# First attention of a graph and feed-forward kernel made ahead of the gathers, five units to four steps, and causal logits made first where it is done

## The chip, the cores and the metric

The kernel runs on one core of a Trainium2 chip, as one program. The metric is device time in microseconds. Five engines work side by side, each through its own list of instructions in order: TensorE (PE in the rows, its weight loads PEld), VectorE (DVE), ScalarE (ACT), GpSimd (POOL, which here issues gathers only) and SyncE (SP, which issues all other transfers). They wait for each other by semaphores.

## The reference, cut to what matters

Four residual layers run over `x`, 2048 nodes of 128 channels: a graph attention with curvature, a product-key feed-forward with causal attention, a second graph attention, and a mixture of experts. The change lies in the first two, which the kernel does in one stage:

```python
x = x + _L0_gnn_ref(_layernorm(x), positions, curv_feats, adj, W, a_l, a_r, Wc, gate)
x = x + _L0_ffn_ref(_layernorm(x)[None], Wq_pk, pk_keys, Wq, keys_table, values_table, Wo)[0]
...
# first: logits over all 2048 nodes for 8 heads, masked by adj, softmax, weigh h
logits = leaky_relu(e_l[:, None, :] + e_r[None, :, :]) + gate * curv_bias
out = einsum('ijh,jhd->ihd', softmax(where(mask, logits, -1e9), axis=1), h)
...
# second: per head, 16 rows of a table of keys and one of values chosen by two top-16 lists,
# summed with softmax weights; then causal attention over the 2048 nodes with them
k = einsum('bnhk,bnhkd->bnhd', kv_scores, keys_table[ind])
v = einsum('bnhk,bnhkd->bnhd', kv_scores, values_table[ind])
attn = softmax(where(causal, einsum('bihd,bjhd->bhij', q, k), neg))
out = einsum('bhij,bjhd->bhid', attn, v)
```

## The kernel before, in words

The stage is the function `curvature_keys_and_attention`. The nodes are cut into 16 tiles of 128 (T = 16), and everything is done for 8 heads (H = 8).

**Units of first attention.** The first attention is cut into 128 units of 16 nodes and all 8 heads (KU = 8 units a tile). A unit u needs: its logits (TensorE, eight matmuls into the four banks of `psL`, L548 and L552), a relu part and a difference (ScalarE, L722 and L729), their sum and row-maximum (VectorE, `max_of`, L863 to L868), the exponential (ScalarE, L734), four rounds of turning (TensorE, L559), copying (ScalarE, L742) and weighing (TensorE, L567), and a scaled pick (VectorE, L873 and L875). The logits of the next unit are made ahead of the weighing of this one. After the eighth unit of a tile the picks are folded and added to X (L629, L1049), the tile is normalised and turned into `row_xT` (L1053 to L1060, L686, L815), and the next block of the adjacency is converted (`turn_adj`, L854).

**Steps of gathering.** From tile 1 on, each step (t, k) also serves head k of tile t - 1: TensorE makes a query (L643) and the similarities (L652), VectorE finds the 16 rows (`choose`, L907 to L968), POOL gathers them, 16 indirect transfers to a step (L508), into a ring that holds two steps' rows. Two steps later (LAG = 2) VectorE sums them with their weights (L993, L997, L1006, L1007). TensorE turns the summed key (L660), and ScalarE copies it (L796). SP stores key and value to device memory.

**Causal attention.** In step x = 12 + w (BEHIND = 12), head w of the causal attention is taken up (w counts 8 heads to a tile): query (L573, copy L756), logits in `psL` (`attend`, L585 and L587) over up to 16 blocks, maximum on VectorE (L880), exponential on ScalarE (L766), and in the next step `at_head`: turning (L592), copying (L749), weighing with the values (L604), then a projection (`project`, L620), which VectorE adds to X (L889). SP fetches the values (L468) and keys (L461) of a head from device memory.

**Order.** The program is written out in full, 18 rounds of `tile` with 8 steps each: 144 steps, x = 8t + k. Rounds 0 to 15 hold first attention, one unit a step; rounds 1 to 16 choose and gather; heads of causal attention lie at steps 12 to 139. So steps 0 to 7 hold first attention alone, and steps 128 to 143 none. No planner orders the work: each engine goes through its own list in the order of its `tile` function, for TensorE in a step with everything: query, logits of the next unit, similarities, causal query, turn of a key, `at_head` of the last head, `attend` of this one, `project`, and turning and weighing of this unit. VectorE: last sums' weights and the first 8 slots, pick of the last unit, maximum of the next, choosing with the causal maximum in it, the other slots.

Of the kernel before, what the change touches and what calls it, by code (L numbers as in the profile page):

```python
# [6 lines left out]
C = 128  # L7
P = 128
T = N // P
H = 8  # L10
# [179 lines left out]
BEHIND = H + LAG + 2  # L190


def curvature_keys_and_attention(nc, ins, X, ident, big_ident, psL, psT, psV, psO, keysT_out, values_out, adj_out):
# [28 lines left out]
    with ExitStack() as ctx:  # L222
# [59 lines left out]
        row_xT = sb("row_xT", [C, 4, P])  # L282
# [135 lines left out]
        with nc.Block() as block:  # L418
            @block.sync
            def _(sp):  # L420
# [49 lines left out]
                def tile(t, s1, last, choosing, adding):  # L470
                    if s1:
                        sp.wait_ge(adj_turned, t + 1)
                        if not last:
                            sp.dma_start(adj_raw[:, :], adj_v[:, t + 1, :]).then_inc(adj_loaded, 16)
                        sp.dma_start(adj_out[t, :, :], adj_neg[:, :]).then_inc(adj_stored, 16)
                    for k in range(H):
# [12 lines left out]
                        if v is not None:  # L489
                            fetch_keys(v)  # L490

                each_tile(tile)
# [20 lines left out]
            def _(pe):  # L513
# [23 lines left out]
                def logits_of(t, k, first=False):  # L537

                    u = KU * t + k
                    if not first:  # L540
                        pe.wait_ge(mx_ready, u)
                    if k == 0:
                        pe.wait_ge(adj_turned, t + 1)
                    v = attended(t, k - 1)
                    if v is not None and v >= 1:
                        pe.wait_ge(at_probs_ready, v)
                    for c in range(NC):
                        nc.tensor.matmul(psL[:, c * CH:(c + 1) * CH], spread[:, k, :],  # L548
                                         adj_neg[:, c * CH:(c + 1) * CH], start=True, stop=False)
                        if c == 0:  # L550
                            pe.wait_ge(diff_ready, u + 1)
                        last = nc.tensor.matmul(psL[:, c * CH:(c + 1) * CH], bias_w[:, :],  # L552
                                                bias_rhs[:, k % 2, c * CH:(c + 1) * CH], start=False, stop=True)
                    last.then_inc(logits_ready, 1)
# [8 lines left out]
                def weigh(t, k, q):  # L563
                    pe.wait_ge(probsT_ready, 4 * (KU * t + k) + q + 1)
                    for s in range(4):
                        j = 4 * q + s
                        last = nc.tensor.matmul(psV[:, k % 2, :], probsT[:, q % 2, s, :], vals[:, j, :],  # L567
# [4 lines left out]
                def query(t, v):  # L572
                    nc.tensor.matmul(psT[:, 1, 2 * NK:2 * NK + P], at_wq[:, v % H, :], row_xT[:, t % 4, :],  # L573
                                     start=True, stop=True).then_inc(at_q_done, 1)

                def attend(v, u):
# [3 lines left out]
                    pe.wait_ge(mx_ready, min(u + 2, UNITS))  # L580
# [15 lines left out]
                def at_weigh(v, q):  # L596
                    pe.wait_ge(at_probsT_ready, quarters_to(v) + q + 1)
                    if q == 0:
# [3 lines left out]
                        pe.wait_ge(x_added, min(T, (v + 1 + BEHIND) // H))  # L602
# [6 lines left out]
                def at_head(v):  # L609
# [3 lines left out]
                    for q in range(n):  # L613
                        if q + 1 < n:
                            at_turn(v, q + 1)
                        at_weigh(v, q)
# [6 lines left out]
                def fold_in(t):  # L623
                    pe.wait_ge(picked_ready, KU * (t + 1))
                    v = attended(t, KU - 1)
                    if v is not None:
                        pe.wait_ge(at_added, v)
# [5 lines left out]
                def tile(t, s1, last, choosing, adding):  # L633
                    for k in range(H):
                        v = H * (t - 1) + k
                        u = KU * t + k
                        w = attended(t, k)
                        if choosing:
                            if k == 0:
                                pe.wait_ge(xT_ready, t)  # L640
                            if not s1:
                                pe.wait_ge(key_copied, v - LAG - 1)
                            nc.tensor.matmul(psT[:, 0, 0:P], wq[:, k, :], row_xT[:, (t - 1) % 4, :],  # L643
                                             start=True, stop=True).then_inc(qT_done, 1)
                        if s1:
                            if k < KU - 1:
                                logits_of(t, k + 1)
                            elif not last:
                                logits_of(t + 1, 0)
                        if choosing:  # L650
                            pe.wait_ge(qT_copied, v + 1)
                            nc.tensor.matmul(psT[:, 1, 0:2 * NK], qT[:, :], keys[:, k, :],  # L652
                                             start=True, stop=True).then_inc(sim_done, 1)
                        if w is not None:
                            query(w // H, w)
                        if turns_key(t, k, choosing, adding):
                            pe.wait_ge(total_ready, v - LAG)
                            if not choosing:
                                pe.wait_ge(key_copied, v - LAG - 1)
                            nc.tensor.transpose(psT[:, 0, 0:P], total[:, :], ident[:, :]).then_inc(key_turned, 1)  # L660
                            pe.wait_ge(key_copied, v - LAG)
                        if choosing:
                            pe.wait_ge(sim_copied, v + 1)
                        if w is not None:
                            pe.wait_ge(at_q_ready, w + 1)
# [5 lines left out]
                        if s1:  # L671
                            pe.wait_ge(probs_ready, u + 1)
                            turn(0)
                            turn(1)
                            if u >= 1:
                                pe.wait_ge(picked_ready, u)
                            weigh(t, k, 0)
                            turn(2)
                            weigh(t, k, 1)
                            turn(3)  # L680
                            weigh(t, k, 2)
                            weigh(t, k, 3)
                    if s1:
                        fold_in(t)
                        pe.wait_ge(xn_ready, t + 1)
# [8 lines left out]
                logits_of(0, 0, first=True)  # L694
                each_tile(tile)
                at_head(H * T - 1)
# [3 lines left out]
            def _(act):  # L700
# [17 lines left out]
                def relu_of(t, k):  # L718
                    u = KU * t + k
                    if u >= 1:  # L720
                        act.wait_ge(probs_ready, u)
                    nc.scalar.activation(relu_part[:, :], er_rows[:, :], ACT.Relu,  # L722
                                         bias=el_cols[:, bass.ds(u, 1)], scale=1.0 - SLOPE).then_inc(relu_ready, 1)

                def diff_of(t, k):
# [968 lines left out]
```

## Time and profile before

| what | value |
|---|---|
| median of 3 runs | 4347.53 us (4346.95 to 4349.38) |
| the profiled execution | 4337.04 us |
| its span, first to last instruction | 4335.3 us |
| busy in the span: TensorE, VectorE, ScalarE, POOL | 3470.9, 3336.2, 2284.3, 2049.0 us |
| mean granted clock of TensorE, of full speed | 0.918 |
| the stage of the change | until about 2998 us |

Busy time is the time in instructions; what an engine spends on issuing transfers, waiting and branching isn't in it, so POOL's share says little about how close its gathers follow one another. A row of a timeline gives the start, the busy time, the engine, the line, the operation and the tiles, the count of the merged instructions, and in brackets the idle time ahead and what ended it. The granted clock is a share of 2.4 GHz; 0.5 is 1.2 GHz, and a value in between is a mean over a stretch that had both.

### The profile page before, as it was taken

How to read it: one execution, taken by the hardware profiler on the slowest of the kernel's cores; microseconds unless marked ns; L12 is line 12 of the kernel's file. 1: busy time of each engine (PE TensorE's matmuls, PEld its weight loads, DVE VectorE, ACT ScalarE, POOL GpSimd, SP SyncE). 2: the span in 40 equal slices, each digit the busy share in tenths (PEclk: the TensorE clock that was granted, in tenths of full speed). 3: DMA queues.
4: the chain of work that ended last, by engine and by line, in shares of the span. 5: the costliest groups of instructions: out<-in, count | busy, mean ns of one | idle time of the engine just before them, and what ended most of it. 6: DMA issues, size and time to landing. Idle time of an engine off the chain costs nothing. (4 is left out here: it accounts for less than half of the span.)

```text
span 4335.3 us, 62381 instructions
## 1 busy us (share of the span) xinstructions
PE 3470.9 (80%) x19465; PEld 2679.8 (62%) x19592; DVE 3336.2 (77%) x10591; ACT 2284.3 (53%) x3657; POOL 2049.0 (47%) x2052
## 2 busy tenths in 40 slices
PE   6867777777778788888888989566888888888797
PEld 4645555555555565566666666445677777777575
DVE  2679889899898898898988989663877777777334
ACT  5645455555555555565555655222656666665232
POOL 0377777777777777777766767660000000000000
PEclk9988889999999999999999999777999999999799
DMA  2244444554555555555555556554000000000100
GB/s 75 61 128 118 133 139 134 146 153 141 156 149 162 168 170 174 170 179 176 180 180 184 189 168 205 171 181 160 1 1 1 1 1 1 1 1 1 41 0 10
DMA packets 187672, 477.90 MB, mean 110 GB/s; under 512 B 43933, under 2 KB 87137, under 8 KB 182881
## 3 DMA queue, kind: packets, MB, share of 16 engines
q0 software_dynamic: 98304, 268.57, 21.4%
q1 hardware_dynamic: 89052, 205.52, 14.0%
q8 instruction: 151, 2.47, 0.2%
q14 instruction: 165, 1.34, 0.1%
HBM read 447.57 MB, written 26.21 MB: 109 GB/s over the span
## 5 line engine op out<-in xcount | busy, mean ns | idle before, releaser
L508 POOL DMA_INDIRECT ck_ring<-in_tables,ck_rows x2048 | 2048.8, 1000 | 879.4 <-issue 751.3
L993 DVE SCALAR_TENSOR_TENSOR ck_part<-ck_ring,ck_norm_w,ck_part 128x256 f32<-128x256 f32 x1792 | 768.7, 475 | 62.5 <-DVE ck_rows L968 41.7
L567 PE MATMUL psV<-ck_vals,ck_probsT 128*128 128x128 f32 x4096 | 554.2, 284 | 112.3 <-ACT ck_probsT L742 105.8
L552 PE MATMUL psL<-ck_bias_rhs,ck_bias_w 110*128 110x512 f32 x1024 | 571.7, 641 | 87.0 <-ACT ck_bias_rhs L729 38.4
L567 PEld LDWEIGHTS psV<-ck_vals,ck_probsT 128*128 128x128 f32 x4096 | 501.8, 196 | 161.3 <-ACT ck_probsT L742 92.0
L1204 PE MATMUL psL<-ga_probsT,ga_vals 128*128 128x256 f32 x2048 | 528.1, 405 | 0.7 <-ACT ga_probsT L1301 0.7
L742 ACT COPY ck_probsT<-psT 128x512 f32<-128x512 f32 x512 | 281.3, 587 | 443.5 <-PE psT L559 439.1
L1204 PEld LDWEIGHTS psL<-ga_probsT,ga_vals 128*128 128x128 f32 x2048 | 398.7, 205 | 51.6 <-ACT ga_probsT L1301 0.9
L1191 PE MATMUL psT<-ident,ga_probs 128*128 128x128 f32 x2048 | 303.0, 283 | 153.8 <-ACT ga_probsT L1301 149.5
L1191 PEld LDWEIGHTS psT<-ident,ga_probs 128*128 128x128 f32 x2048 | 248.8, 146 | 204.4 <-issue 184.1
L1292 ACT ACTIVATE ga_probs<-ga_probs,ga_neg_mx 128x2048 f32<-128x2048 f32 x128 | 256.5, 2004 | 220.9 <-DVE ga_neg_mx L1352 220.5
L1301 ACT COPY ga_probsT<-psT 128x512 f32<-128x512 f32 x512 | 281.3, 585 | 162.9 <-PE psT L1191 162.3
L585 PE MATMUL psL<-ck_keysT,ck_at_qT 128*128 128x512 f32 (+3 forms) x640 | 270.5, 555 | 91.7 <-DVE ck_neg_mx L868 91.5
L604 PE MATMUL psO<-ck_at_probsT,ck_values 128*128 128x128 f32 x2176 | 308.2, 291 | 41.5 <-ACT ck_at_probsT L749 41.5
L604 PEld LDWEIGHTS psO<-ck_at_probsT,ck_values 128*128 128x128 f32 x2176 | 276.3, 201 | 71.2 <-ACT ck_at_probsT L749 71.2
L552 PEld LDWEIGHTS psL<-ck_bias_rhs,ck_bias_w 110*128 110x128 f32 x1024 | 213.1, 208 | 165.5 <-issue 145.6
L559 PE MATMUL psT<-ident,ck_probs 128*128 128x128 f32 x2048 | 305.4, 285 | 3.1 <-ACT ck_sim L786 2.7
L1342 DVE SCALAR_TENSOR_TENSOR ga_probs<-ga_s_rows,ga_s_cols,ga_s_slope 128x2048 f32<-128x2048 f32 x128 | 300.3, 2346 | 6.6 <-ACT ga_s_slope L1274 6.0
L1346 DVE CUSTOM_DVE_ANT_0 ga_probs<-ga_probs,ga_adj_neg 128x2048 f32<-128x2048 f32 x128 | 292.6, 2286 | 5.4
L864 DVE CUSTOM_DVE_ANT_0 ck_relu_part<-psL,ck_relu_part 128x2048 f32<-128x2048 f32 x128 | 292.8, 2287 | 0.5 <-issue 0.5
L749 ACT COPY ck_at_probsT<-psT 128x512 f32<-128x512 f32 (+3 forms) x320 | 159.0, 524 | 206.3 <-PE psT L592 206.3
L734 ACT ACTIVATE ck_probs<-ck_relu_part,ck_neg_mx 128x2048 f32<-128x2048 f32 x128 | 257.8, 2014 | 16.1 <-DVE ck_neg_mx L868 16.1
(205 smaller groups left out, 5616.0 us busy)
## 6 DMA issues: line engine op xcount, KB each, us to landing
ck_ring<-in_tables,ck_rows POOLq DMA_INDIRECT x2048
ck_adj_raw<-in_adj SPq DMA_DIRECT2D x16, 1024.0 KB, 9.5
adj_scratch<-ck_adj_neg SPq DMA_DIRECT2D x16, 512.0 KB
values_scratch<-ck_values_tile SPq DMA_DIRECT2D x128, 64.0 KB, 1.7
keysT_scratch<-ck_keys_tile SPq DMA_DIRECT2D x128, 64.0 KB
ck_keysT<-keysT_scratch SPq DMA_DIRECT2D x8, 1024.0 KB
ck_values<-values_scratch SPq DMA_DIRECT2D x8, 1024.0 KB
ga_adj_neg<-adj_scratch SPq DMA_DIRECT2D x16, 512.0 KB, 11.9
```

What stands on the lines that cost most here:

```text
L508: pool.indirect_dma_start(ring[:, slot, :], None, ins["tables"], bass.IndirectOffsetOnAxis(rows[:, k, s:s + 1], axis=0)).then_inc(got[(u * ...
L552: last = nc.tensor.matmul(psL[:, c * CH:(c + 1) * CH], bias_w[:, :], bias_rhs[:, k % 2, c * CH:(c + 1) * CH], start=False, stop=True)
L559: last = nc.tensor.transpose(psT[:, q % 2, s * P:(s + 1) * P], probs[:, j * P:(j + 1) * P], ident[:, :])
L567: last = nc.tensor.matmul(psV[:, k % 2, :], probsT[:, q % 2, s, :], vals[:, j, :], start=(j == 0), stop=(j == T - 1))
L604: last = nc.tensor.matmul(psO[:, P:2 * P], values[:, j, :], at_probsT[:, q % 2, j % 4, :], start=(j == 0), stop=(j == blocks(v) - 1))
L742: nc.scalar.copy(probsT[:, q % 2, :, :].rearrange("p s c -> p (s c)"), psT[:, q % 2, :]).then_inc(probsT_ready, 1)
L864: nc.vector.tensor_tensor_reduce(out=logits[:, :], in0=psL[:, :], in1=relu_part[:, :], scale=1.0, scalar=-3.0e38, op0=ALU.add, op1=ALU.max ...
L993: done.append(c.did(nc.vector.scalar_tensor_tensor(part[:, s % 2, :], ring[:, slot, :], norm_w[:, s:s + 1], part[:, s % 2, :], ALU.mult, A ...
L1191: last = nc.tensor.transpose(psT[:, q % 2, s * P:(s + 1) * P], probs[:, u % 3, j * P:(j + 1) * P], ident[:, :])
L1204: last = nc.tensor.matmul(out, vals[:, k % 2, j, :], probsT[:, g % 2, j, :, :].rearrange("p h i -> p (h i)"), start=(j == 0), stop=(j == T ...
L1342: nc.vector.scalar_tensor_tensor(probs[:, u % 3, :], s2_rows[:, k % 2, :], s1_cols[:, t, k:k + 1], s2_slope[:, k % 2, :], ALU.add, ALU.max ...
L1346: nc.vector.tensor_tensor_reduce(out=probs[:, u % 3, :], in0=probs[:, u % 3, :], in1=adj_neg[:, t, :], scale=1.0, scalar=-3.0e38, op0=ALU.add,
```

## The change: what it does

- The order is written over units instead of tiles. Round 0 is as before. In rounds 1 to 16 each fourth step is followed by an extra unit, which does first attention alone, as long as units are left. So five units of first attention go to four steps of gathering; the last unit (127) is the extra one behind step 103, and steps 104 to 143 have none.
- Where a step has no first attention (`g is None`), TensorE makes the causal logits of this head (`attend`) right behind the causal query, ahead of the turn of the key and of `at_head` of the last head. In the other steps the order is as before.
- Normalised tiles are kept eight deep (`KEPT`) instead of four, since they are made further ahead.
- SP loads and stores an adjacency block behind the unit that ends a tile, instead of ahead of the next tile's first step.
- Columns of the biases are read at constant places instead of through a register's slice. `opening` is False throughout, so what hangs on it is not done.

```diff
+EVERY = 4
+KEPT = 8
...
-        row_xT = sb("row_xT", [C, 4, P])
+        row_xT = sb("row_xT", [C, KEPT, P])
...
-        def each_tile(tile):
-
-            for t in range(T + 2):
-                tile(t, s1=t < T, last=t >= T - 1, choosing=1 <= t <= T, adding=2 <= t <= T + 1)
+        def each_unit(unit):
+
+            g = 0
+            for x in range(H * (T + 2)):
+                t, k = x // H, x % H
+                unit(t, k, g if g < UNITS else None, choosing=1 <= t <= T, adding=2 <= t <= T + 1, extra=False)
+                g = min(g + 1, UNITS)
+
+                if 1 <= t <= T and x % EVERY == EVERY - 1 and g < UNITS:
+                    unit(t, k, g, choosing=False, adding=False, extra=True)
+                    g += 1
...
+                def keep_adj(j):
+                    sp.wait_ge(adj_turned, j + 1)
+                    if j + 1 < T:
+                        sp.dma_start(adj_raw[:, :], adj_v[:, j + 1, :]).then_inc(adj_loaded, 16)
+                    sp.dma_start(adj_out[j, :, :], adj_neg[:, :]).then_inc(adj_stored, 16)
...
+                    if g is not None and g % KU == KU - 1 and g + 1 < UNITS:
+                        keep_adj(g // KU + 1)
...
-                        pe.wait_ge(x_added, min(T, (v + 1 + BEHIND) // H))
+                        if folds(g) >= 1:
+                            pe.wait_ge(x_added, folds(g))
...
+                def unit(t, k, g, choosing, adding, extra):
+                    v = H * (t - 1) + k
+                    w = None if extra else attended(t, k)
+                    issued = (attended(t, k) or 0) + (1 if extra and attended(t, k) is not None else 0)
+                    more = g is not None and g + 1 < UNITS
+                    opening = False
+                    if folds(g) >= 1:
+                        pe.wait_ge(xT_ready, folds(g))
+                    if choosing:
+                        if g is None:
+                            pe.wait_ge(key_copied, v - LAG - 1)
+                        nc.tensor.matmul(psT[:, 0, 0:P], wq[:, k, :], row_xT[:, (t - 1) % KEPT, :],
+                                         start=True, stop=True).then_inc(qT_done, 1)
+                    if more and not opening:
+                        logits_of(g + 1, issued)
+                    if choosing:
+                        pe.wait_ge(qT_copied, v + 1)
+                        nc.tensor.matmul(psT[:, 1, 0:2 * NK], qT[:, :], keys[:, k, :],
+                                         start=True, stop=True).then_inc(sim_done, 1)
...
+                    if w is not None:
+                        query(w // H, w)
+                    if w is not None and g is None:
+                        attend(w, g)
+                    if turns_key(t, k, choosing, adding):
+                        pe.wait_ge(total_ready, v - LAG)
...
+                    if w is not None:
+                        pe.wait_ge(at_q_ready, w + 1)
+                        if g is None:
                             if w >= 1:
-                                at_head(w - 1)
-                            attend(w, u)
+                                at_head(w - 1, g)
+                        else:
                             if w >= 1:
-                                project(w - 1)
...
+                                at_head(w - 1, g)
+                            attend(w, g)
+                        if w >= 1:
+                            project(w - 1)
+                    if g is not None:
+                        pe.wait_ge(probs_ready, g + 1)
+                        turn(0)
+                        turn(1)
+                        if g >= 1:
+                            pe.wait_ge(picked_ready, g)
+                        weigh(g, 0)
...
+                    if g is not None and g % KU == KU - 1:
+                        fold_in(g // KU, attended(t, k))
...
+                    if summing is not None:
+                        norm_weights(*summing)
+                        add_slots(TOP - BESIDE if g is not None else 2)
+                    if g is not None and g % KU >= 1:
+                        pick(g - 1)
+                    if more and not opening:
+                        max_of(g + 1)
+                    w = None if extra else attended(t, k)
```

The lists of ScalarE and VectorE follow the same loop: in an extra unit ScalarE does relu, difference, four copies and an exponential, VectorE a pick and a maximum, and where a unit ends a tile, the tile's end as before.

## Rows read from the trace of the kernel before

**Rows 1.** Windows of the stage; columns: PE, PEld, DVE, ACT, POOL, PEclk, DMA share, GB/s

```profile
161.00:2170.00 2009.00, 1578.83 (x8786) 1163.66 (x8881) 1780.95 (x6630) 1096.28 (x1824) 1523.23 (x1518) 0.93 0.51 153
2170.00:2712.00 542.00, 477.26 (x2844) 357.15 (x2867) 473.08 (x1676) 317.09 (x511) 381.36 (x384) 0.97 0.57 185
2712.00:2907.00 195.00, 115.53 (x542) 90.06 (x540) 135.55 (x508) 49.49 (x109) 128.76 (x132) 0.72 0.54 178
```

**Rows 2.** Timeline of POOL, its last two gathers

```profile
2926.45 0.95 POOL L508 DMA_INDIRECT ck_ring<-in_tables,ck_rows  x1 [0.30 <-issue]
2927.71 0.95 POOL L508 DMA_INDIRECT ck_ring<-in_tables,ck_rows  x1 [0.30 <-issue]
```

**Rows 3.** Line L508, all gathers: who waited for them (us, times)

```profile
  DVE ck_part L993: 20.7, 12
```

**Rows 4.** Timeline of VectorE in an ordinary step

```profile
1232.57 0.15 DVE L873 RECIPROCAL ck_rinv<-ck_rsum 128x1 f32<-128x1 f32 x1
1233.03 2.29 DVE L864 CUSTOM_DVE_ANT_0 ck_relu_part<-psL,ck_relu_part 128x2048 f32<-128x2048 f32 x1
...
1235.44 0.49 DVE L907 MAX8 ck_best<-ck_sim 128x8 f32<-128x128 f32 x2
...
1252.54 2.28 DVE L864 CUSTOM_DVE_ANT_0 ck_relu_part<-psL,ck_relu_part 128x2048 f32<-128x2048 f32 x1
```

**Rows 5.** Timeline of TensorE in the same step

```profile
1223.69 2.05 PE L567 MATMUL psV<-ck_vals,ck_probsT 128*128 128x128 f32 x16 [1.35 <-ACT ck_probsT L742]
...
1229.26 1.02 PE L552 MATMUL psL<-ck_bias_rhs,ck_bias_w 110*128 110x512 f32 x2
```

**Rows 6.** Timeline of TensorE in tile 0, a unit with nothing beside it

```profile
104.92 1.02 PE L552 MATMUL psL<-ck_bias_rhs,ck_bias_w 110*128 110x512 f32 x2
...
109.02 1.04 PE L559 MATMUL psT<-ident,ck_probs 128*128 128x128 f32 x8
...
115.17 1.02 PE L552 MATMUL psL<-ck_bias_rhs,ck_bias_w 110*128 110x512 f32 x2
```

**Rows 7.** Timeline of VectorE, row-maxima of four units around a tile's end

```profile
933.61 2.29 DVE L864 CUSTOM_DVE_ANT_0 ck_relu_part<-psL,ck_relu_part 128x2048 f32<-128x2048 f32 x1
...
957.72 2.29 DVE L864 CUSTOM_DVE_ANT_0 ck_relu_part<-psL,ck_relu_part 128x2048 f32<-128x2048 f32 x1
...
986.60 2.29 DVE L864 CUSTOM_DVE_ANT_0 ck_relu_part<-psL,ck_relu_part 128x2048 f32<-128x2048 f32 x1
...
1005.68 2.29 DVE L864 CUSTOM_DVE_ANT_0 ck_relu_part<-psL,ck_relu_part 128x2048 f32<-128x2048 f32 x1
```

**Rows 8.** Timeline of VectorE, rows chosen in step 103 and in step 135

```profile
2169.59 1.04 DVE L968 TENSOR_REDUCE ck_rows<-ck_hit 128x16 uint32<-128x864 f32 x1
...
2906.62 1.04 DVE L968 TENSOR_REDUCE ck_rows<-ck_hit 128x16 uint32<-128x864 f32 x1
```

**Rows 9.** Timeline of a step without first attention, VectorE and TensorE

```profile
2783.93 2.16 DVE L880 TENSOR_REDUCE ck_at_neg_mx<-psL 128x1 f32<-128x1920 f32 x1 [6.15 <-PE psL L587]
...
2795.25 0.47 PE L660 MATMUL psT<-ident,ck_total 128*128 128x128 f32 x1 [5.25 <-DVEq L173]
...
2796.13 1.97 PE L592 MATMUL psT<-ident,ck_at_probs 128*128 128x128 f32 x8 [0.41 <-ACT ck_keys_tile L796]
...
2802.67 3.39 PE L585 MATMUL psL<-ck_keysT,ck_at_qT 128*128 128x512 f32 x8
...
2806.15 2.16 DVE L880 TENSOR_REDUCE ck_at_neg_mx<-psL 128x1 f32<-128x1920 f32 x1 [4.53 <-PE psL L587]
```

**Rows 10.** Timeline of SP's queue in the same step

```profile
2802.91 0.32 SPq L468 DMA_DIRECT2D ck_values<-values_scratch  x1
...
2806.19 0.32 SPq L461 DMA_DIRECT2D ck_keysT<-keysT_scratch  x1
```

**Rows 11.** Window of one microsecond, columns as in rows 1

```profile
2813.00:2814.00 1.00, 0.00 (x0) 0.00 (x0) 0.97 (x3) 0.10 (x1) 0.59 (x1) 0.50 0.12 45
```

**Rows 12.** Timeline of VectorE, the stage's last addition to X

```profile
2997.09 0.35 DVE L889 SCALAR_TENSOR_TENSOR X<-psO,ck_at_rinv,X 128x128 f32<-128x128 f32 x1 [9.40 <-PE psO L620]
```

More of the change, by code:

```diff
@@ L468, in fetch_values @@
                     sp.dma_start(values[:, 0:n, :], values_out[v % H, :, 0:n, :]).then_inc(values_in, 16)
[L470 to L476, printed above, removed]
+                def keep_adj(j):
[4 more added lines that the diff above has]
+                def unit(t, k, g, choosing, adding, extra):
+                    if not extra:
                         n = H * t + k - (BEHIND - 1)
@@ L631, in fold_in @@
                     last.then_inc(folded, 1)
[L633 to L665, printed above, removed]
@@ L693, in _ @@
                 pe.wait_ge(at_in, 48)
-                logits_of(0, 0, first=True)
-                each_tile(tile)
-                at_head(H * T - 1)
+                logits_of(0)
+                each_unit(unit)
+                at_head(H * T - 1, None)
                 project(H * T - 1)
@@ L822, in _ @@
+                        nc.scalar.copy(row_xT[:, g // KU % KEPT, :], psT[:, 0, 0:P]).then_inc(xT_ready, 1)
+                relu_of(0)
+                diff_of(0)
+                diff_of(1)
+                exp_of(0)
+                each_unit(unit)
                 at_copy(H * T - 1)
@@ L855, in turn_adj, with max_of @@
                                             ALU.is_gt, ALU.add).then_inc(adj_turned, 1)
[L857 to L859 removed]
+                def max_of(u):
+                    if u >= 1:
                         dve.wait_ge(probs_ready, u)
@@ new lines, in unit, with add_slots, attend_now @@
+                def unit(t, k, g, choosing, adding, extra):
+                    more = g is not None and g + 1 < UNITS
+                    opening = False
+                    if more and g % KU == KU - 1:
+                        turn_adj(g // KU + 1)
+                    summing = summed(t, k, choosing, adding)
+                    done = []
+                    def add_slots(n):
+                        if summing is not None:
+                            for s in range(len(done), min(len(done) + n, TOP)):
+                                add_slot(*summing, s, done)
+                    if summing is not None:
[5 more added lines that the diff above has]
+                        max_of(g + 1)
+                    w = None if extra else attended(t, k)
+                    def attend_now():
+                        if w is not None:
+                            attend(w)
+                    if choosing:
+                        choose(t - 1, k, not adding and k == 0, add_slots, summing is not None, attend_now)
+                    else:
+                        attend_now()
+                    if more and opening:
+                        max_of(g + 1)
+                    if summing is not None:
+                        add_slots(TOP)
+                        finish_sums(*summing, adding or k > LAG, done)
+                    if g is not None and g % KU == KU - 1:
+                        tile = g // KU
+                        pick(g)
+                        dve.wait_ge(folded, tile + 1)
+                        nc.vector.tensor_tensor(X[:, tile, :], X[:, tile, :], psO[:, 0:P], ALU.add).then_inc(x_added, 1)
+                        dve.wait_ge(x_added, tile + 1)
@@ L1064, in _ @@
                 dve.wait_ge(keys_in, 64)
-                max_of(0, 0, first=True)
-                each_tile(tile)
+                max_of(0)
+                each_unit(unit)
                 add_head(H * T - 1)
```

245 lines of the change are left out of this document (102 added, 143 removed).

## The prediction

> **What bounds the kernel now.** I read the stages first, by windows [rows 1]. The change touches the stage up to 2998 us and nothing behind it. For most of that stage, 161 to 2170 us, VectorE is busy 1781 us of 2009 (89%), TensorE 1579 (79%), ScalarE 1096 (55%), and POOL 1523 (76%). POOL's share misleads: the gap between two gathers isn't counted as busy. Start to start, two gathers in a row are 1.26 us apart [rows 2], so 16 cost about 20.1 us without a pause. A step (one gathered head) takes some 21 us on average. POOL is therefore nearly full too. But who waits for whom? VectorE waited for a gather only 20.7 us in the whole run, in 12 places [rows 3]. So it is VectorE's own order, not POOL, that sets the pace of most steps, with POOL close behind it.
>
> Inside an ordinary step VectorE has no hole worth naming: from one row-maximum (L864) at 1233.03 to the next at 1252.54 is 19.5 us [rows 4]. TensorE is ahead of it there: its last weighing ends at 1223.69 + 2.05 = 1225.7, the next unit's logits are done at 1229.26 + 1.02 = 1230.3, and VectorE comes for them only at 1233.03 [rows 4, 5]. TensorE is thus 2.8 us early, no more.
>
> **Part 1: 24 units of first attention without a gather.** From step 8 on, five units go to four steps, so the 120 units that are left after tile 0 take 96 steps and 24 extra passes. What an extra pass costs is seen in tile 0, where units run with nothing beside them: logits start at 104.92, turning at 109.02, the next unit's logits at 115.17 [rows 6], that is 10.25 us of TensorE for a unit, 4.1 for logits and 6.15 for turning and weighing, with ScalarE's copies between. An extra pass puts these 10.25 us in TensorE's order behind the weighing at 1225.7, at 1236.0; the step's own logits need 4.5 us behind that (1225.7 to 1230.3), so the row-maximum that was at 1233.03 comes at 1240.5, 7.5 us later. VectorE's extra work (pick and maximum, 1232.57 to 1235.44, 2.9 us [rows 4]) fits into that. ScalarE's share of such a unit does too: it kept up with the 10.25 us in tile 0, and 55% leave it room. Bounds: 2.9 us, if only VectorE's work counted, and 10.25, if TensorE had no lead. I take 7.5, as rows 4 to 6 give it directly: 24 x 7.5 = +180 us.
>
> **Part 2: tile ends come earlier.** Every eighth unit ends a tile: fold, layer norm, turning, a new adjacency block. Row-maxima around one are at 933.61, 957.72, 986.60 and 1005.68 [rows 7]: 24.1 and 28.9 us against 19.1 of the plain step behind them, so 14.8 us for a tile's end, most of it waiting (VectorE's fold, norm and adjacency block are short). Before, step 103 had begun the end of tile 12 (counted from 0); now all sixteen are over by then. Three and two thirds of an end move ahead of step 104: +54 us here, and they come off the stretch of part 3, whose old time holds them. Bounds: 0, if extra passes filled all of it, and 54.
>
> **Part 3: steps 104 to 135 carry no first attention.** Their rows came from 2169.59 to 2906.62 [rows 8], 737.0 us or 23.0 a step. In the last eight of them, which had no first attention before either, a step takes 2806.15 - 2783.93 = 22.2 us, of which VectorE waits 4.5 to 6.2 for causal logits [rows 9]. The chain there: sums done, key turned at 2795.25, at_head (turn and weigh) from 2796.13, logits from 2802.67, maximum at 2806.15. The second part of the change takes the logits ahead of the key's turning, so VectorE no longer waits: its own work is 22.2 - 4.5 = 17.7 us. Who is late next? POOL, at 20.1 us a step; and a new loop: keys are fetched right behind the values once weighing ends (2802.91 before, the keys at 2806.19 [rows 10]). The two transfers are over by 2813, where the DMA's share has fallen to 0.12 [rows 11], 10.2 us after the weighing. Add logits (3.4), key turn and copy (0.9) and at_head (6.5): 21.0 us at 15 blocks, less with fewer. Bounds: 20.1 (POOL) and 22.2 (no gain). I take 21.0: 32 x 21.0 = 672, so -65 us. Queued behind the logits' new place are the key's turn, at_head and project, and ScalarE and SP wait for these; that wait is in the loop.
>
> **Part 4: the ends.** At the start VectorE's 20.7 us of waiting for gathers [rows 3] lie in the first steps, where two or three extra passes fall: -21 (bounds 0 and -21). Behind the last gather (2927.71 [rows 2]) the stage runs on to 2997.09 [rows 12], 69 us in which VectorE waits for causal logits; the new order shortens each of four heads by a few us: -10 (bounds 0 and -24). SP's adjacency load and store now stand behind a step's four transfers instead of ahead of them; what they wait for is done by then, and the next block is needed six steps later: 0. Eight kept row blocks in place of four, and constants in place of a register for the columns: 0, no wait of before names them.
>
> **The sum:** 180 + 54 - 21 - 65 - 10 = **+138 us**. The profiled execution took 4337.0 us (span 4335.3 and 1.7 around it), so 4475; the runs' median of 4347.5 is 10.5 above that execution, so **4485 us** on the runs.
>
> **Rivals.** *Cheap passes.* TensorE's pass might hide wholly, so that an extra unit costs VectorE's 2.9 us alone: 24 x 2.9 = 70 in place of 180, +28, 4376 us. For it: VectorE is the busiest engine [rows 1]. Against: TensorE's lead is 2.8 us and the pass takes 10.25 [rows 4 to 6]. The Trainium skill, Perfetto Trace Analysis, "Identifying the Most-Contended Engine", says that the engine with the highest occupancy is the one that limits; by that rule this rival would hold, and the trace agrees with it only for plain steps. 13%.
>
> *VectorE never waits (faster).* As the last, and the waits at tile ends are filled as well, since an extra pass now stands beside some of them: ends cost 0 in place of 54, sum 70 - 21 - 65 - 10 = -26, 4321 us. The place is VectorE's wait between the last weighing of a tile and the next maximum. It decides if an extra pass with its share of a tile's end costs under (21 + 65 + 10) / 24 = 4.0 us; I have 9.8. For it: up to 14.8 us at each end [rows 7]. Against: TensorE's order is fixed, and only three extra passes stand directly ahead of the last unit of a tile. 7%.
>
> *TensorE alone in the freed steps is slow.* The granted clock is 0.72 in the stretch without first attention against 0.93 and 0.97 ahead of it [rows 1], a mixture of 1.2 and 2.4 GHz; eight transposes take 1.97 us here [rows 9] and took 1.04 in tile 0 [rows 6]. If the loop of part 3 runs at the lower, its 10 us of TensorE grow by several, the freed steps gain only what was bounded above (-26), the tail nothing, and if TensorE's lead is used up elsewhere the passes cost 10.25: 246 + 54 - 21 - 26 = +253, 4600 us. The Trainium skill, TensorE: Matmul & The Clock Gate, "Part 1: The HAM clock gate (the 'warmup' mystery)", calls the half rate the default that only activity lifts; that speaks against taking work away from TensorE, and the rows of this stretch agree. 15%.
>
> *It does not do what it says.* Excluded: 8 + 5 x 24 = 128 units by step 103, written out by the program's own loop.
>
> **How the numbers follow.** My own case has 65%, and its range is 4430 to 4540 (an extra pass at 6 to 9 us, freed steps at 20.1 to 22). The range must hold 8 in 10: down to the cheap passes, and up into the slow case: 4370 to 4580. About 0.2% (8.7 us) is what a measurement of this kernel can tell from no change. Faster needs the second rival: 7%. Within 0.2% needs something between the first rival and the second: 4% of the 13% of cheap passes. The rest, 65 + 15 + 9 = 89%, is slower.
>
> **What would show it.** Right: in steps 8 to 103 VectorE waits 3 to 5 us for psL by L552's line in each extra pass, POOL shows pauses for rows (L971's queue) where it had none, and gathers end later than 2927.7 by some 150 us; from step 104 on POOL runs again nearly without pause, and the wait for L587's line is gone. Wrong: no wait of VectorE in an extra pass (cheap passes), or steps of 22 us and more after 104 with waits for keys (slow case). If POOL stays without pauses up to step 103, the sum falls at part 1.

## The result and the profile after

| | before | after |
|---|---|---|
| median of the runs, us (4 each, side by side) | 4347.92 (4346.95 to 4349.38) | 4465.52 (4461.28 to 4468.62) |
| span of the profiled execution | 4335.3 | 4464.5 |
| its own time | 4337.0 | 4466.2 |
| rows chosen in step 103 | 2169.59 | 2375.14 |
| rows chosen in step 135 | 2906.62 | 3035.16 |
| last gather starts | 2927.71 | 3078.27 |
| last addition to X | 2997.09 | 3128.57 |

The changed kernel is slower: its time is 1.027 times that of before (95% interval 1.0252 to 1.0287), 118 us. 4485 was forecast, with 4370 to 4580 as the range.

The page of the changed kernel: the span, the engines' busy time and the gathers.

```profile
span 4464.5 us, 62417 instructions
...
PE 3527.0 (79%) x19465; PEld 2680.7 (60%) x19592; DVE 3339.3 (75%) x10591; ACT 2284.9 (51%) x3657; POOL 2048.3 (46%) x2052
...
L525 POOL DMA_INDIRECT ck_ring<-in_tables,ck_rows x2048 | 2048.1, 1000 | 1030.7 <-issue 761.2
```

The work is the same, 2048 gathers of 1000 ns on average; what grew is the idle time between them. Where it grew, the windows by stage show (columns as in [rows 1]; the stages end where step 103, step 135 and the stage end now).

```profile
161.00:2375.00 2214.00, 1806.29 (x10209) 1333.56 (x10327) 1856.21 (x6806) 1287.81 (x2020) 1514.24 (x1518) 0.94 0.47 140
2375.00:3036.00 661.00, 422.44 (x1979) 286.06 (x1977) 538.38 (x2023) 178.64 (x424) 500.37 (x499) 0.78 0.59 193
3036.00:3129.00 93.00, 59.38 (x295) 41.73 (x295) 30.67 (x67) 21.78 (x39) 33.48 (x33) 0.78 0.42 146
```

POOL has some 1515 us of gathers up to step 103, as before [rows 1], in 2214 us in place of 2009. In the stretch without first attention it is busy 500 us of 661 (76%), which is close to no pause at all, as [rows 2] said.

VectorE's timeline in the changed kernel, the choice of rows (L992, L968 before) in steps 23, 103, 104 and 135, then the last addition to X:

```profile
486.80 1.04 DVE L992 TENSOR_REDUCE ck_rows<-ck_hit 128x16 uint32<-128x864 f32 x1
...
2375.14 1.05 DVE L992 TENSOR_REDUCE ck_rows<-ck_hit 128x16 uint32<-128x864 f32 x1
...
2405.58 1.05 DVE L992 TENSOR_REDUCE ck_rows<-ck_hit 128x16 uint32<-128x864 f32 x1
...
3035.16 1.05 DVE L992 TENSOR_REDUCE ck_rows<-ck_hit 128x16 uint32<-128x864 f32 x1
...
3128.57 0.35 DVE L913 SCALAR_TENSOR_TENSOR X<-psO,ck_at_rinv,X 128x128 f32<-128x128 f32 x1 [10.50 <-PE psO L636]
```

Against [rows 8] and [rows 12]: step 103 comes 205.5 us later, step 135 only 128.5 later, and the stage ends 131.5 later. So 205.5 us go to steps 8 to 103, 77 come back in steps 104 to 135, and 3 go to what follows. Of the 205.5, 2.1 were there before the first extra unit: the rows of step 8 are chosen at 165.07 in the profiled execution of before and at 167.20 in this one.

**An extra pass.** VectorE's row-maxima (L888) about an ordinary extra unit of the changed kernel, the one behind step 55; the second is the one that VectorE makes in the extra unit:

```profile
1215.55 2.29 DVE L888 CUSTOM_DVE_ANT_0 ck_relu_part<-psL,ck_relu_part 128x2048 f32<-128x2048 f32 x1
...
1232.00 0.06 DVE L887 MEMSET ck_waited<- 128x1 f32 x1 [0.58 <-PE psL L567]
1232.04 2.29 DVE L888 CUSTOM_DVE_ANT_0 ck_relu_part<-psL,ck_relu_part 128x2048 f32<-128x2048 f32 x1
...
1242.46 0.06 DVE L887 MEMSET ck_waited<- 128x1 f32 x1 [4.10 <-PE psL L567]
1242.51 2.29 DVE L888 CUSTOM_DVE_ANT_0 ck_relu_part<-psL,ck_relu_part 128x2048 f32<-128x2048 f32 x1
```

The stretch takes 27.0 us with the extra unit in it. Row-maxima of plain steps are 19.1 to 19.5 us apart [rows 4, 7], so this unit cost 7.5 to 7.9 us. TensorE over the same time:

```profile
1225.47 2.05 PE L582 MATMUL psV<-ck_vals,ck_probsT 128*128 128x128 f32 x16 [1.22 <-ACT ck_probsT L762]
1227.57 1.02 PE L567 MATMUL psL<-ck_bias_rhs,ck_bias_w 110*128 110x512 f32 x2
...
1231.67 1.04 PE L574 MATMUL psT<-ident,ck_probs 128*128 128x128 f32 x8
1233.03 1.13 PE L582 MATMUL psV<-ck_vals,ck_probsT 128*128 128x128 f32 x8 [0.33 <-ACT ck_probsT L762]
...
1235.77 2.00 PE L582 MATMUL psV<-ck_vals,ck_probsT 128*128 128x128 f32 x16
...
1238.04 1.02 PE L567 MATMUL psL<-ck_bias_rhs,ck_bias_w 110*128 110x512 f32 x2
```

From one unit's logits (1227.57) to the next's (1238.04) it is 10.47 us with hardly a hole; the pass was costed at 10.25 from [rows 6]. VectorE, 2.8 us behind TensorE in the plain step [rows 4, 5], now waits for it, here 0.58 + 4.10 us. ScalarE does not hold the pass up: TensorE waits 0.33 us for one of its copies, and its copies wait 2.35 us for TensorE (0.35, 1.26 and 0.74). All such waits up to step 103, first before, then after (columns: who waits, for what; us in total, times, longest):

```profile
DVE ck_waited L863 <- PE psL L552: 78.8, 23, 5.5
...
POOL ck_ring L508 <- DVEq L992: 36.2, 64, 5.4
```

```profile
POOL ck_ring L525 <- DVEq L1016: 250.6, 79, 20.4
...
DVE ck_waited L887 <- PE psL L567: 207.7, 62, 8.5
```

VectorE waits 129 us longer for first logits, and POOL, which had no pause to speak of, stands 214 us longer behind VectorE's queue: the two signs that the prediction named for part 1. It named the line that hands over rows for the second one (L971, now L995), and the trace puts the pauses down to the line that frees places of the ring (L1016). The gather that ends a long pause starts 2.0 us behind a choice of rows, though (step 56: rows at 1254.0, and the gather at 1256.0, 5.3 us behind the one before it).

**A freed step.** Steps 104 to 135 run differently: TensorE, VectorE and POOL of the changed kernel in one of them.

```profile
2869.46 5.10 PE L600 MATMUL psL<-ck_keysT,ck_at_qT 128*128 128x512 f32 x8 [0.76 <-DMA ck_keysT<-keysT_scratch]
```

```profile
2880.18 0.62 DVE L1021 TENSOR_SCALAR ck_part<-ck_ring,ck_norm_w 128x256 f32<-128x256 f32 x2 [4.69 <-DMA ck_ring<-in_tables,ck_rows]
```

```profile
2877.54 0.95 POOL L525 DMA_INDIRECT ck_ring<-in_tables,ck_rows  x1 [0.30 <-issue]
2878.80 0.94 POOL L525 DMA_INDIRECT ck_ring<-in_tables,ck_rows  x1 [0.30 <-issue]
2880.04 0.95 POOL L525 DMA_INDIRECT ck_ring<-in_tables,ck_rows  x1 [0.30 <-issue]
```

VectorE now waits for gathers (4.69 us at 2880), where it waited for causal logits before [rows 9]. In these rows POOL issues one every 1.25 us without a hole. The waits of steps 104 to 135:

```profile
PE psL L600 <- DMA ck_keysT<-keysT_scratch: 67.6, 26, 5.7
...
DVE ck_part L1021 <- DMA ck_ring<-in_tables,ck_rows: 50.4, 23, 4.7
```

From step 104 to 135 it is 3035.16 - 2405.58 = 629.6 us in 31 steps, 20.3 each. The gathers are slower than these choices of rows. The first gather of step 104 and the first of step 135:

```profile
2407.59 0.98 POOL L525 DMA_INDIRECT ck_ring<-in_tables,ck_rows  x1 [9.20 <-DVEq L995]
...
3057.72 2.46 POOL L525 DMA_INDIRECT ck_ring<-in_tables,ck_rows  x1 [0.30 <-issue]
```

That is 650.1 us, 21.0 for 16 gathers, with no wait of POOL above 0.3 us in between. The rows of step 104 were chosen 2.0 us ahead of its first gather, those of step 135 22.6 us ahead: VectorE gained a lead of some 21 us, most of it in the first eight steps (18.4 us each, 21.0 in the 23 behind them).

### The profile page after: what moved, and what is told of

It is laid out like the page before. It is cut to its first block and busy times, and to the rows that moved or that the text cites. A ratio compares the mean times of both kernels' runs of the same rounds, so it can differ in the third digit from the quotient of the medians.

```text
span 4464.5 us, 62417 instructions
## 1 busy us (share of the span) xinstructions
PE 3527.0 (79%) x19465; PEld 2680.7 (60%) x19592; DVE 3339.3 (75%) x10591; ACT 2284.9 (51%) x3657; POOL 2048.3 (46%) x2052
## 5 line engine op out<-in xcount | busy, mean ns | idle before, releaser
L600 PE MATMUL psL<-ck_keysT,ck_at_qT 128*128 128x512 f32 (+3 forms) x640 | 344.1, 680 | 159.9 <-DMA ck_keysT<-keysT_scratch 97.7
L600 PEld LDWEIGHTS psL<-ck_keysT,ck_at_qT 128*128 128x128 f32 x640 | 142.4, 241 | 314.2 <-issue 207.4
L620 PE MATMUL psO<-ck_at_probsT,ck_values 128*128 128x128 f32 x2176 | 294.2, 282 | 45.4 <-ACT ck_at_probsT L769 45.4
L620 PEld LDWEIGHTS psO<-ck_at_probsT,ck_values 128*128 128x128 f32 x2176 | 262.5, 192 | 75.4 <-ACT ck_at_probsT L769 75.4
L888 DVE CUSTOM_DVE_ANT_0 ck_relu_part<-psL,ck_relu_part 128x2048 f32<-128x2048 f32 x128 | 293.0, 2289 | 0.2 <-issue 0.2
L574 PEld LDWEIGHTS psT<-ident,ck_probs 128*128 128x128 f32 x2048 | 254.2, 149 | 21.7 <-issue 17.1
```

The source lines that it names most:

```text
L574: last = nc.tensor.transpose(psT[:, q % 2, s * P:(s + 1) * P], probs[:, j * P:(j + 1) * P], ident[:, :])
L600: nc.tensor.matmul(psL[:, c * CH:c * CH + w * P], at_qT[:, :], keysT[:, 4 * c:4 * c + w, :], start=True, stop=4 * c + w < n)
L620: last = nc.tensor.matmul(psO[:, P:2 * P], values[:, j, :], at_probsT[:, q % 2, j % 4, :], start=(j == 0), stop=(j == blocks(v) - 1))
L888: nc.vector.tensor_tensor_reduce(out=logits[:, :], in0=psL[:, :], in1=relu_part[:, :], scale=1.0, scalar=-3.0e38, op0=ALU.add, op1=ALU.max ...
```

## The experiments

The theory was the prediction's: an extra unit costs what its TensorE pass takes beyond TensorE's lead, and the new order makes the freed steps cheaper. The rivals: VectorE's extra work sets the cost; every extra unit costs the same wherever it stands; something else of the change (kept blocks, SP's adjacency transfers behind the step's own) has a price. Each kernel was timed in three rounds beside the kernel before.

### Neither part: the frame alone

```
-EVERY = 4
+EVERY = 10 ** 6
...
-                    if w is not None and g is None:
-                        attend(w, g)
...
-                        if g is None:
-                            if w >= 1:
-                                at_head(w - 1, g)
-                        else:
-                            if w >= 1:
-                                at_head(w - 1, g)
-                            attend(w, g)
+                        if w >= 1:
+                            at_head(w - 1, g)
+                        attend(w, g)
```

> The changed kernel without extra units and without the logits made first; what is left of the change is the eight kept row blocks, SP's adjacency transfers behind the unit, and constants for the columns. My theory: these cost nothing, about 4348 us as before (within 0.2%). Rival: they carry a part of the loss of 118 us, then 4360 us or more.

Measured: 4346.45 us against 4347.17, ratio 0.9999 (0.9986 to 1.0011). The frame costs nothing, as part 4 said. So the two parts carry the whole change.

### Logits first, no extra units

```
-EVERY = 4
+EVERY = 10 ** 6
```

> Only the second part: no extra units, causal logits first in steps without first attention (128 to 143). My theory: steps 128 to 135 go from 23.9 us to the 20.3 that the changed kernel shows in such steps, eight times 3.6 less what their first step keeps of a tile's end, the tail unchanged: 20 to 25 us faster than before, 4325 us. Rival: the freed steps of the changed kernel are quick only because gathers had been left behind and VectorE ran ahead, then no gain, 4348 us.

Measured: 4324.0 us, ratio 0.9946 (0.9928 to 0.9963), a gain of 23 us with only eight steps to gain in. VectorE's waits for causal logits fall from 115.9 us (34 times) to 49.0 (24 times) in the whole run. It is the better half of the change.

### Extra units, causal logits in their old place

```
-                    if w is not None and g is None:
-                        attend(w, g)
...
-                        if g is None:
-                            if w >= 1:
-                                at_head(w - 1, g)
-                        else:
-                            if w >= 1:
-                                at_head(w - 1, g)
-                            attend(w, g)
+                        if w >= 1:
+                            at_head(w - 1, g)
+                        attend(w, g)
```

> Only the first part: 24 extra units, but causal logits behind at_head as before. My theory: steps 8 to 103 as in the changed kernel, steps 104 to 135 at about 22 us in place of 20.2, so 50 to 60 us slower than the changed kernel, 4515 to 4525 us. Rival: the gathers limit these steps anyway, then the same as the changed kernel, 4466 us.

Measured: 4528.77 us, ratio 1.0416 (1.0399 to 1.0434): 182 us above the frame alone, and 63 above the changed kernel. So the second part is worth 63 us when 32 steps use it and 23 when eight do. Its stretch behind step 103, in the windows (columns as in [rows 1]), and VectorE's waits for causal logits in the whole run:

```profile
2374.00:3100.00 726.00, 414.36 (x1974) 325.22 (x1972) 535.91 (x2022) 181.85 (x424) 516.12 (x515) 0.73 0.55 180
```

```profile
DVE ck_at_neg_mx L898 <- PE psL L602: 210.0, 45, 13.5
```

726 us here, 661 in the changed kernel; 210.0 us of waits for logits here, 24.6 there. Taking units ahead without the new order gains only 11 us on the 737.0 of [rows 8].

### VectorE's share of an extra unit made 2.1 us longer

```
                         max_of(g + 1)
+                        if extra:
+                            for again in range(2):
+                                c.did(nc.vector.tensor_tensor(hit[:, :, :], hit[:, :, :],
+                                                              cand_row[:, :].unsqueeze(1).to_broadcast([P, TOP, CAND]),
+                                                              ALU.mult))
+                                dve.wait_ge(step, c.count)
```

> The changed kernel with two more VectorE passes of 1.05 us in each extra unit, behind its maximum (their result is never read). My theory: TensorE's 10.25 us set an extra unit and VectorE stands idle over 3 us in each, so nothing changes: 4466 us, within 8. Rival (the busiest engine, VectorE, sets it): 24 times 2.1 more, 4516 us.

Measured: 4463.97 us, ratio 1.0266 (1.0249 to 1.0283), the changed kernel's own time. VectorE's timeline, its waits up to step 103 and the group of the added operation:

```profile
2375.31 1.05 DVE L992 TENSOR_REDUCE ck_rows<-ck_hit 128x16 uint32<-128x864 f32 x1
```

```profile
DVE ck_waited L887 <- PE psL L567: 160.8, 61, 8.5
```

```profile
L1059 DVE TENSOR_TENSOR ck_hit<-ck_hit,ck_cand_row 128x864 f32<-128x864 f32 x46 | 48.5, 1055 | 0.8
```

48.5 us of work more on the busiest engine, 46.9 us fewer of waiting (207.7 to 160.8), and step 103 where it was, within 0.2 us (2.4 us later if counted from the rows of step 8, which are at 165.01 here). VectorE's work, up to these 2.1 us more, does not set what an extra unit costs. The Trainium skill, Perfetto Trace Analysis, "Identifying the Most-Contended Engine", takes the engine with the highest occupancy as the one to work on. By busy time that is VectorE here, with 84% of the stretch up to step 103 (1856 of 2214 us), and this run shows that it had room where the extra units stand.

### TensorE's share of an extra unit made shorter

Extra units turn and weigh two of their four blocks per round; half of these units' weighing is left out.

```
-                        turn(0)
+                        n = 2 if extra else 4
+                        turn(0, n)
...
-                        weigh(g, 0)
+                        weigh(g, 0, n)
```

> The changed kernel, but in the 24 extra units TensorE turns and weighs only half of the columns (two of four blocks in each round), which leaves half of these units' weighing out of the result; VectorE's and ScalarE's work is as it was. My theory: TensorE's pass is what an extra unit costs, and it gets about 2 us shorter (the chain of turning, copying and weighing limits the gain): 24 times 2, 4415 us. Rival (VectorE or ScalarE set it): 4466 us.

Measured: 4415.16 us against 4344.74, ratio 1.017 (1.0153 to 1.0187); in medians 50 us below the changed kernel, 43 by the ratios to the kernel before in each one's own rounds. VectorE's timeline, rows of step 103:

```profile
2322.96 1.04 DVE L993 TENSOR_REDUCE ck_rows<-ck_hit 128x16 uint32<-128x864 f32 x1
```

Step 103 comes 52.2 us earlier than in the changed kernel, 2.3 us for each of the 23 extra units ahead of it. In the unit behind step 55 it is 8.5 us from one unit's logits to the next's (1201.51 to 1209.98), where it was 10.47. A shorter pass on TensorE pays, longer work on VectorE costs nothing: the cost lies in TensorE's order.

### Extra units only ahead of a tile's last unit

```
-                if 1 <= t <= T and x % EVERY == EVERY - 1 and g < UNITS:
+                if 1 <= t <= T and g % KU == KU - 2 and g < UNITS:
```

> Extra units only ahead of the last unit of a tile (15 of them instead of 24, steps 8 to 112), logits first as in the changed kernel. My theory: there a pass of TensorE fills a wait that was there anyway, and costs 2.8 us as the trace of the changed kernel shows it, against 8.0 elsewhere: 15 times 2.8 on top of 4325, less about 1 us for each of 15 more freed steps, 4350 to 4360 us. Rival (every extra unit costs the same 7.5 to 8 us): 4420 to 4440 us.

Measured: 4355.48 us, ratio 1.003 (1.0017 to 1.0042). VectorE's timeline, rows of step 103:

```profile
2233.20 1.04 DVE L992 TENSOR_REDUCE ck_rows<-ck_hit 128x16 uint32<-128x864 f32 x1
```

That is 63.6 us later than before, with 13 extra units and 1.67 ends of tiles more by then. At the 14.7 us of an end in the prediction the ends are 24.5, so 39.1 is left, 3.0 per unit: about VectorE's 2.9 [rows 4]. That TensorE's pass fits there into the wait that VectorE has at the tile's end in any case is argued from this number. This is the place that the "VectorE never waits" rival named, and it exists; but it has room for one unit a tile, and the change put three of its 24 there.

### Logits first, no extra units, keys fetched ahead of values

The logits' new place leaves TensorE waiting for keys, which SP fetches behind the values, and those behind a weighing. In steps without first attention SP now fetches the next head's keys first.

```
-                        if v is not None:
+                        if v is not None and g is not None:
                             fetch_values(v)
...
                             fetch_keys(v)
+                        v = attended(t, k)
+                        if v is not None and g is None:
+                            fetch_values(v)
```

> No extra units, logits first, and in steps without first attention SP fetches the next head's keys ahead of this head's values, so that they don't wait for the weighing. My theory: in the last steps and the tail TensorE waits for keys that are fetched too late, 6 us a step; this wait goes and the tail gets shorter: 10 to 25 us below the run with the logits first alone, about 4308 us. Rival: the values are then late in their place, or the gathers limit all of it: no difference, 4325 us.

Measured: 4297.03 us against 4344.74, ratio 0.9893 (0.9876 to 0.9911), 27 us below the run without the swap in medians (23 by the ratios to the kernel before in each one's own rounds): faster than both kernels. Behind the last gather the stage ran on for 68.7 us in the run with logits first alone (2917.64 to 2986.37) and for 39.0 here (2916.38 to 2955.38). The last head's fetches and logits in the run with logits first alone, SP's queue and TensorE:

```profile
2953.80 0.32 SPq L481 DMA_DIRECT2D ck_values<-values_scratch  x1
2954.24 0.36 SPq L474 DMA_DIRECT2D ck_keysT<-keysT_scratch  x1
```

```profile
2961.05 6.21 PE L600 MATMUL psL<-ck_keysT,ck_at_qT 128*128 128x512 f32 x8 [6.25 <-DMA ck_keysT<-keysT_scratch]
```

and in this run:

```profile
2924.06 0.32 SPq L474 DMA_DIRECT2D ck_keysT<-keysT_scratch  x1
```

```profile
2933.30 3.67 PE L603 MATMUL psL<-ck_keysT,ck_at_qT 128*128 128x512 f32 x8 [1.46 <-ACT ck_at_qT L779]
```

The keys are asked for 30 us earlier, TensorE no longer waits for them, and the last head's logits begin 27.8 us earlier. Behind the last gather three sets of causal logits are left in the run with logits first alone (at 2921.51, 2941.12 and 2961.05) and one here.

### The changed kernel, keys fetched ahead of values

The same edit of SP's order, on the changed kernel.

> The changed kernel with the next head's keys fetched ahead of this head's values in steps 104 to 143. My theory: TensorE's 98 us of waiting for keys go, but in steps 104 to 130 the gathers limit, so only the last steps and the tail gain: 10 to 25 us, 4448 us. Rival (the wait for keys sets all freed steps): 50 us or more, 4415 us or less.

Measured: 4455.87 us, ratio 1.0261 (1.0244 to 1.0278). The interval overlaps that of the changed kernel, so the runs alone do not tell them apart; in the profiled executions the last addition to X comes 9.5 us earlier (3119.05), the last gather in the same place (3078.91 against 3078.27). TensorE's waits for keys are all but gone (one of 1.6 us on its weight load, from step 104 on), and the gathers keep their 21.0 us a step (first gather of step 104 at 2408.36, of step 135 at 3059.81). So TensorE's 67.6 us of waits for keys in the freed steps cost nothing there: the gathers cover them. What the swap gains shows behind the last gather.

## Why the prediction was right

It forecast +138 us on the profiled execution; that rose by 129. By its parts:

**Part 1 (24 passes at 7.5)** held, in mechanism and size. Step 103 comes 203.4 us later, counted from step 8, with 23 extra units and 2.67 ends of tiles more; without the ends (39) 164 are left, 7.1 a unit. From step 23 to step 103 alone it is 186.5 us with 20 units and two ends (29.4), 7.9 a unit. The number is a mean: an ordinary extra unit costs some 8.0 (with no end of a tile near, choices of rows around one are 25.7 to 29.7 us apart from step 15 on, and 18.7 to 20.2 next to it), one ahead of a tile's last unit about 3. The "cheap passes" rival falls with the run in which VectorE did 2.1 us more per unit at no cost. The "VectorE never waits" rival needed less than 4.0 us for a pass with its share of an end; it was 8.8 (203.4 / 23).

**Part 2 (3.67 ends, +54)** was not tried by itself. The sum up to step 103 agrees with it, and its pieces come off steps 104 to 135 again.

**Part 3 (672 us for steps 104 to 135)** had the pace right and the reason wrong. By the gathers the 31 steps behind step 104 take 21.0 us each, as forecast, but what sets them is POOL and not the keys' loop: with the keys fetched first TensorE's waits go and the gathers keep their 21.0. That the loop was costed at the same 21.0 is chance. The prediction put POOL at 20.1 from two gathers in a row; over these 496 a gather starts 1.31 us behind the last on average, single ones up to 2.1 us. The loop is there (TensorE waits for keys 26 times), but it runs beside the gathers. By the choices of rows the stretch took 660.0 us, and in the prediction's count it is 672 + 7.5 + 14.7 = 694, as the 24th unit and one end of a tile fell into it, which it had counted ahead of step 104. Of these 34 us too much, 13 lie between step 103 and 104: 30.4 us, where 21.0 + 7.5 + 14.7 = 43.2 were counted. The last unit has no logits and no maximum of a next one to make; that this is the reason is not shown. The other 21 are the lead that VectorE's choices gained over the gathers. It is no time won by itself: the last gather now starts 43.1 us behind the last choice of rows, where it was 21.1 before.

**Part 4 (start -21)** was half right. At step 23, with three extra units done, the rows come 19.0 us later (486.80 against 467.82), 16.9 counted from step 8. The units (8 + 8 + 3 by the costs above) and the 0.67 of a tile's end that is over earlier (9.8) would be 28.8, so some 12 us were absorbed and not 21. VectorE's waits for gathers did go, from 17.4 to 2.9 us between 160 us and step 23, and its waits for first logits rose from 7.4 to 23.4 in the same steps: one wait took the other's place in part. Why not more was absorbed was not tried further.

**Part 4 (tail -10)**: behind the last gather the stage ran on for 50.3 us in place of 69.4, so -19, inside the bounds of 0 and -24. The tail goes with the number of causal logits that begin behind the last gather: three before and with logits first alone (69.4 and 68.7 us), two in the changed kernel (50.3), one in the two runs with keys fetched first (39.0 and 40.1). The new order alone did not shorten it. The lead of the choices goes with it (22 us with logits first alone, 43 in the changed kernel); that this lead is the cause is argued and not shown.

**The sum.** Against the forecast of 138: +2 were there before step 8; the first steps +6 (22.5 + 9.8 - 21 = 11.3 in the prediction's count, 16.9 measured); passes and ends from step 24 to 103 +7 (179.4, and 186.5); the stretch behind -34; and from step 135 on +13, as 3 us were lost there (93.4 us to the last addition, 90.5 before) where 10 were to be gained. That makes 132, against 131.5 at the last addition to X and 129 in the span. Counted at the last gather instead, which does not see the lead of the choices, 148 were forecast and 150.6 came, and behind it -10 and -19. That the sum came so near is in part luck: 15 us too little up to step 103 and 13 too much in the step behind it cancelled.

**From the execution to the runs** 10.5 us were added, since the profiled execution of before lay that far below its runs' median. The one of after lies 0.7 above its own. Single runs of the kernel before lay between 4336.75 and 4356.69 in all comparisons, so that the 10.5 was where one execution happened to fall.

**The rival of a slow TensorE** was half right. The granted clock is 0.78 in steps 104 to 135 (0.72 before in the stretch without first attention [rows 1], 0.73 in the run with extra units alone), again a mixture of 1.2 and 2.4 GHz. Eight matmuls of causal logits take 5.10 us in the step shown, where the prediction put 3.4 from [rows 9]. The Trainium skill, TensorE: Matmul & The Clock Gate, "Part 1: The HAM clock gate (the 'warmup' mystery)", says that the rate is halved until activity lifts it. This stretch, from which work of TensorE was taken, agrees in that. The lower clock cost nothing in the freed steps, since POOL had no wait there. What the clock costs behind the last gather no run here tells apart from the waits for keys.

## What to carry to other kernels

Work that is taken out of one stage and put into another is priced in the stage that receives it, along the engine whose order it lengthens: here the in-order pass of TensorE, 10.5 us less the little lead it had, and not the busy share of the busiest engine. When a wait is removed, look for the resource that issues without a pause (here the gathers) before a new loop is priced, since a loop that runs beside it costs nothing until that resource is done. Take its pace from many issues in a row: two gathers gave 20.1 us a step, 496 gave 21.0. And when one half of a change moves work and the other shortens a chain, try each alone: here the small half won 23 us, 48 with the fetches in the matching order, and the large half lost 182.

## What the runs showed of the hardware

With first attention gone, 496 gathers in a row started 1.31 us apart on average (21.0 us for 16), 1.00 us of it shown as busy and 0.30 us put down to issue, whether TensorE waited for keys or not (21.0 with the keys fetched first). The median distance is 1.25 us. POOL shows 77% busy over these gathers (499.1 of 650.2 us) and had no wait above 0.3 us between them, so it was full.

The same eight matmuls (128x512) took longer the lower the granted clock was. Windows of one such group each, in the kernel before [rows 9], in the tail with logits and keys first, and in the tail of the changed kernel:

```profile
2802.70:2806.10 3.40, 3.40 (x12) 1.61 (x11) 0.00 (x0) 0.27 (x1) 2.67 (x3) 1.00 0.71 217
...
2910.80:2916.20 5.40, 5.39 (x9) 2.04 (x9) 2.85 (x8) 0.00 (x0) 4.12 (x4) 0.68 0.67 253
...
3040.70:3047.40 6.70, 6.70 (x10) 2.73 (x10) 3.33 (x10) 0.00 (x0) 5.08 (x6) 0.54 0.42 117
```

They took 3.4 us with 1.00 granted, 5.4 with 0.68 and 6.7 with 0.54. The first stands right behind other work of TensorE, the second behind 1.46 us of waiting for a query, the third behind 8.4 us of waiting for keys. The wait for keys is not all that lowers the clock here: in the steps without first attention of the run with keys first, where TensorE has no wait for them, such groups took 4.9 to 6.7 us too (at 2802.43, 6.7 us with 0.54 granted).
